# Layer-norm epsilon folded into VectorE's statistics, two biases moved from GpSimd adds into matmul accumulation, and all four engine orders rewritten, in a two-layer token tower

## What is computed

```python
h = concat(cls, patches @ W.T + b) + pos_enc                                   # tokens
x = ln(h); n = ln(x) * gamma + beta                                            # two norms, one after the other
z, c = sigmoid(n @ Wg.T + bg), n @ Wc.T + bc
h = h + scan(s = (1 - z) * s + z * c over an image's tokens) + x               # gated scan
h = h + (ln(gelu(ln(h) @ ternary(W_fc).T)) * ln_w + ln_b) @ ternary(W_proj).T  # first FFN
x = ln(h); q, k = rope(x @ Wq.T + bq), rope(x @ Wk.T + bk); v = x @ Wv.T + bv
h = h + (softmax(causal(q k / 16)) @ v) @ Wf.T + bf                            # attention
h = h + clip(round(ln(h) / scale)) * scale @ (ternary_weight - 1).T + bias     # quantized FFN
```

## Time and profile before

| | us |
|---|---|
| median of 3 runs | 164.12 |
| lowest, highest | 163.8, 164.88 |
| the profiled execution's own time | 163.71 |
| its span, first to last instruction | 161.9 |

### The profile page before, as it was taken

How to read it: one execution, slowest core, us unless ns; L and a number is a source line. 1 busy time by engine, 2 the same in 40 slices (tenths; PEclk the granted TensorE clock), 3 DMA queues, 4 the chain that set the end, 5 groups by cost and what they waited for, 6 DMA issues and landing times.

```text
span 161.9 us, 3532 instructions
## 1 busy us (share of the span) xinstructions
PE 148.2 (91%) x1043; PEld 129.5 (80%) x1043; DVE 136.1 (84%) x396; ACT 109.0 (67%) x264; POOL 120.3 (74%) x214
## 2 busy tenths in 40 slices
PE   7979999999998999999999999999999999697541
PEld 7969999788997887879888989988998798574220
DVE  0767679999999999999979799888988896896871
ACT  3765359736448899999998958498827637276330
POOL 1068978968927466878889988869899888988830
PEclk9999999999999999999999999999999999999955
DMA  5999992000030000000000000000000000001323
GB/s 171 340 392 392 379 417 109 4 0 2 0 130 4 2 0 2 0 4 0 0 4 2 0 4 0 2 0 0 4 0 0 0 6 2 2 10 46 87 81 81
DMA packets 6026, 10.84 MB, mean 67 GB/s; under 512 B 1841, under 2 KB 3448, under 8 KB 5752
## 3 DMA queue, kind: packets, MB, share of 16 engines
q1 hardware_dynamic: 6008, 10.62, 18.7%
HBM read 9.40 MB, written 1.21 MB: 66 GB/s over the span
## 4 chain that ended last, share of the span: by engine, by line
PE 70%; POOL 13%; DVE 6%; issue 6%; ACT 2%; DVEq 0%; ACTq 0%; POOLq 0%
PE bank L428 37%; PE bank L508 5%; PE bank L575 5%; PE bank L509 4%; PE bank L510 4%; PE bank L517 3%; POOL small L1186 3%; PE bank L435 3%; POOL qk L1251 2%; POOL small L1181 2%; POOL residual L1282 2%; POOL small L1191 2%; PE bank L549 1%; PE bank L629 1%; DVE residual L1160 1%
## 5 line engine op out<-in xcount | busy, mean ns | idle before, releaser
L1186 POOL TENSOR_TENSOR small<-small,powers 111x1 f32<-111x1 f32 (+3 forms) x55 | 33.3, 606 | 3.7
L1181 POOL TENSOR_SCALAR small<-small 111x1 f32<-111x1 f32 (+1 forms) x55 | 24.2, 441 | 15.0 <-DVE small L892 11.3
L428 PE MATMUL bank<-pj,gt_hi 128*111 128x256 f32 (+1 forms) x88 | 22.3, 293 | 0.0
L428 PE MATMUL bank<-pj,gt_lo 128*111 128x256 f32 (+1 forms) x88 | 21.3, 281 | 0.0
L1202 POOL TENSOR_TENSOR x_lo<-x_raw,x_hi 128x666 fp32r<-128x666 f32 (+1 forms) x9 | 12.8, 1434 | 10.8 <-ACT x_hi L721 10.8
L508 PE MATMUL bank<-wt_hi,x_hi 128*111 128x256 f32 (+1 forms) x66 | 19.4, 294 | 1.4 <-DVE h L998 1.1
L510 PE MATMUL bank<-wt_hi,x_lo 128*111 128x256 f32 (+1 forms) x66 | 18.6, 282 | 0.0
L509 PE MATMUL bank<-wt_lo,x_hi 128*111 128x256 f32 (+1 forms) x66 | 18.6, 282 | 0.0
L428 PE MATMUL bank<-fc,n1t_hi 128*111 128x512 f16 (+1 forms) x44 | 16.7, 380 | 0.0
L428 PE MATMUL bank<-fc,n1t_lo 128*111 128x512 f16 (+1 forms) x44 | 16.6, 378 | 0.0
L428 PEld LDWEIGHTS bank<-pj,gt_hi 128*111 128x111 f32 (+1 forms) x88 | 15.1, 171 | 0.3 <-DVE residual L1088 0.2
(11 more groups left out here) (139 smaller groups left out, 478.9 us busy)
## 6 DMA issues: line engine op xcount, KB each, us to landing
x_raw<-x_in SPq DMA_DIRECT2D x10, 333.0 KB, 6.4
w_fc<-w_fc_in SPq DMA_DIRECT2D x1, 1024.0 KB, 10.2
w_pj<-w_pj_in SPq DMA_DIRECT2D x1, 1024.0 KB, 12.2
out_dram<-residual SPq DMA_DIRECT2D x10, 96.0 KB, 1.7
w_tok<-w_tok_in SPq DMA_DIRECT2D x2, 384.0 KB, 4.1
w_gate<-w_gate_in SPq DMA_DIRECT2D x1, 512.0 KB, 5.8
w_qk<-w_qk_in SPq DMA_DIRECT2D x1, 512.0 KB, 7.0
ln_w<-ln_w_in SPq DMA_DIRECT2D x1, 512.0 KB, 3.5
```

The lines of the kernel that those rows point to most:

```text
L428: last = mm(out, a, b, start=(n == 0), stop=(n == len(pairs) - 1))
L1181: return nc.gpsimd.tensor_scalar(small[0:rows(i), i, out:out + 1], small[0:rows(i), i, value:value + 1], factor, add, ALU.mult, ALU.add)
L1186: return gt(small[0:rows(i), i, r:r + n], small[0:rows(i), i, ve:ve + n], powers[0:rows(i), 0:n], ALU.pow)
```

## The change

Four parts.

1. **Epsilon.** The statistics of a tile are six numbers, two groups of (count, mean, sum of squares). The tile `stats` becomes 12 wide, with two more groups of count 0 and mean 0 that POOL writes once at the start (`w_tok` on POOL: six memsets), whose sum of squares is 256 times epsilon. The aggregate reads nine numbers instead of six, and its variance is then variance + epsilon. `scaled` is gone for all norms: five instructions a tile on POOL. Norm 0 has two aggregates on DVE instead of one (`MV0_SQ`, `MV0`), one with e*e/(1 + e) and one with e; the factor 1/sqrt(1 + e) that is left goes into gamma (`w_gamma`, one small DVE instruction, for which `w_gate` on ACT and DVE waits). For norm 3, `NB3` is made of the mean, `R3` and -1/scale, and no longer waits for `RQ`.
2. **Value bias.** The tile `pick` (128 x 112) is 0 but for rows 0 and 32, which are 1. `value_rows` has the bias in all rows, rounded to fp32r, and in row 32 what the rounding left. Their product, 128 rows deep and 256 columns, is the first of now seven matmuls of `value:i`. `vbias` is gone on POOL, and DVE's `attend` doesn't wait for it. Two more instructions in `w_value_bias` on DVE.
3. **Output bias.** `out:i` on PE has the same product with `out_rows` (bias / scale) ahead of its two matmuls: three. `biased` is gone on POOL, and DVE's `out` doesn't wait for it. `w_out_bias` on POOL makes the rows once, in three instructions, after `h1:1`.
4. **Orders.** All four lists of `ORDER` are new. `w_pos:0` is behind `tok:0` on PE in both.

```diff
-                pairs = []
+                pairs = [(pick[0:STACK, 0:rows(i)], value_rows[0:STACK, :])]
...
+                mm(out[0:n, 0:D], pick[0:STACK, 0:n], out_rows[0:STACK, :], start=True, stop=False)
                 for k in range(KD):
-                    last = mm(out[0:n, 0:D], q3t[:, k, span(i)], w_out[:, k, :], start=(k == 0), stop=(k == KD - 1))
+                    last = mm(out[0:n, 0:D], q3t[:, k, span(i)], w_out[:, k, :], start=False, stop=(k == KD - 1))
...
-                    nc.vector.bn_aggr(col(i, normed[norm][2], 2), stats[0:rows(i), norm, i % 2, 0:6])\
-                        .then_inc(s[f"mv{norm}_ready"], 1)
+                    groups = stats[0:rows(i), norm, i % 2, :]
+                    if norm == 0:
+                        nc.vector.bn_aggr(col(i, MV0_SQ, 2), groups[:, 0:3 * GROUP]).then_inc(s["mv0_ready"], 1)
+                        nc.vector.bn_aggr(col(i, MV0, 2), groups[:, 0:4 * GROUP]).then_inc(s["mv0_ready"], 1)
+                    else:
+                        nc.vector.bn_aggr(col(i, normed[norm][2], 2), groups[:, 0:3 * GROUP])\
+                            .then_inc(s[f"mv{norm}_ready"], 1)
...
             def attend(i):
                 n = rows(i)
                 pool.wait_ge(s["mv3_ready"], i + 1)
-                scaled(i, VE3, MV3 + 1, 1.0, LN_EPS).then_inc(s["ve3_ready"], 1)
-                pool.wait_ge(s["ve3_ready"], i + 1)
-                power(i, VE3, R3).then_inc(s["r3_ready"], 1)
+                power(i, MV3, R3).then_inc(s["r3_ready"], 1)
...
-            def biased(i):
-                n = rows(i)
-                pool.wait_ge(s["s3_ready"], i + 1)
-                if i == 0:
-                    pool.wait_ge(s["dma_bias"], 16)
-                gt(res[0:n, i, :], res[0:n, i, :], out_bias[0:n, :], ALU.add).then_inc(s["biased_ready"], 1)
...
@@ the end of PE's list @@
-        turn:10 value:10 out:2 attend:10 out:3 out:4 t3:7 out:5 out:6 out:7 t3:8 out:8 t3:9 out:9 t3:10 out:10""",
+        out:3 turn:10 t3:5 out:4 t3:6 attend:10 t3:7 out:5 out:6 out:7 t3:8 out:8 t3:9 out:9 t3:10 out:10""",
```

More of the change, by code:

```diff
@@ new lines @@
+        tg:12 fc:17 t2:3 tg:13 fc:18 value:0 qk:0 tg:14 qk:1 tg:15 tg:16 fc:19 proj:6 t2:4 qk:2 tg:17 proj:7
+        t1:10 qk:3 tg:18 fc:20 t2:5 t2:6 proj:8 value:1 tg:19 t2:7 fc:21 score:0 score:1 qk:4 qk:5 tg:20 turn:0
+        proj:9 attend:0 qk:6 score:2 tg:21 turn:1 score:3 qk:7 value:2 turn:2 attend:1 t2:8 proj:10 value:3
+        value:4 t2:9 score:4 attend:2 score:5 turn:3 t2:10 value:5 attend:3 turn:4 qk:8 score:6 attend:4 qk:9
+        t3:0 turn:5 value:6 attend:5 turn:6 qk:10 score:7 attend:6 qk:11 value:7 t3:1 turn:7 out:0 t3:2 attend:7
@@ L322, in tower @@
     powers = m.own("powers", [2], F32)
-    stats = m.own("stats", [4, 2, 8], F32)
+    stats = m.own("stats", [4, 2, GROUP * GROUPS], F32)
     squares = m.own("squares", [HID], F16)
```

243 lines of the change are left out of this document (140 added, 103 removed).

## The result

| | median, us | lowest to highest, us | executions |
|---|---|---|---|
| before | 163.79 | 163.2 to 164.88 | 14 |
| changed | 163.0 | 161.93 to 165.76 | 14 |

The ratio is 0.9942, with a 95% interval of 0.9917 to 0.9967: 0.95 us faster (0.0058 x 163.79), where 1.8 were forecast. It is inside the range, and in the class "within 1%", which had a chance of 0.40 where "faster by over 1%" had 0.47. Executions more than 1.5% above their kernel's fastest stay out of every ratio in this document, while medians and ranges are of all executions, and since the profiled execution of the changed kernel was such a one (165.76 us), the profile after is that of its second run (first experiment), with a span of 160.8 us against 161.9.

The account below looks back on a forecast made before the run. PE was taken as the bound to about 130 us (with DVE up to 52), then a latency tail with POOL on the path. +0.8 + 1.75 - 1.6 - 2.7 = -1.8 us: 162.3 on the median, range 160.4 to 165.3.

Parts of the forecast that it names:

- Up to `attend:3`, +1.75: From 52 us to `attend:3`, PE without gaps: two more value stages, one score less, six bias products; +1.75 us.
- `attend:3` to `attend:10`, 18.8: In the tail on DVE: 17.8 us of work plus 1.0 idle, 18.8 instead of 20.4; -1.6 us.
- `attend:10` to the end, 9.2: The end: 3.9 us to the last `round`, 2.6 to the last `out`, 2.7 for stores; 9.2 instead of 11.9, -2.7.
- the hold on `clip`: In the tail: DVE's two `clip` took 1.60 us beside POOL's output adds; without them about 0.5.
- The first stage, +0.8: Up to about 52 us, new order and added DVE work: a loss between 0 and 1.7 us, taken as 0.8.
- two spots: In the first stage: PE waits 1.3 us at `t0:7`; `h1:0` behind its scan is 1.7 us late in all.
- the sign: Check for the first stage: right if PE's gaps between 30 and 52 us grow by about 0.8.
- the lock as a rival: DVE's `fc` and `pj` steps from about 31 us hold POOL's x_lo; PE stands 3.9 us; 165.4 us, chance 0.17.
- Its part on what is removed: 55 epsilon instructions and 22 adds leave POOL: worth nothing from 52 to 112 us, paying in the tail only.
- Another wait: Rival: the tail's idle stays at 3.8 us because another wait replaces POOL's; +1.05, 165.2 us, chance 0.18.
- Packs fully: Rival: the first stage loses 0.2, tail idle falls to 0.3, the end gives 3.1; -3.5, 160.6 us, chance 0.2.
- `w_out_bias`: On POOL after `h1:1`, near 53 us: at most 2.5 us long, costing nothing, up to 1 us if late.

Follow-up runs that it names:

- first experiment: The changed kernel run again with no edit, for a profile of an undisturbed execution: 163.03 us, ratio 0.995 to before.
- the old head: The changed code with all stages up to the first `t1` in the order of before, the later ones in the new order: 162.82 us, ratio 0.983.
- `code_old_order_new`: The kernel before with its own code, its lists replaced by the changed kernel's and the bias additions placed one or two tiles behind their norm: 175.94 us, ratio 1.075.

## Why the prediction was right, and where it was not

- **Up to `attend:3`, +1.75.** Measured +1.05 from `proj:0`. The parts that rows could check agree: the bias product at a spacing of 0.12, and no gap of PE. What made it 0.7 less was not looked for; in that stretch PE's order is different too, and part of the first stage's loss may be taken back there (`h1:0` was 4.15 us late and `proj:0` 3.16).
- **`attend:3` to `attend:10`, 18.8.** Measured 18.2. The idle time was forecast at 1.0 and is 1.1. DVE's work was forecast at 17.8 and is 17.06.
- **`attend:10` to the end, 9.2.** Measured 8.8. The forecast counted the last product at the low clock; the granted clock is 1.00 up to 158 us here, past that product (157.29), and from the end of the last `round` (156.29) to that of the last `out` (158.19) it is 1.9 us where 2.6 were counted. That the hold on `clip` would go was seen rightly.
- **The first stage, +0.8: this is the step that failed**, with +3.2 at `proj:0` (2.7 counted from `tok:1`). The prediction looked at two spots. Both have a wait: 0.51 us at `t0:7` and 0.64 at the scan, with 0.21 at the value bias 1.36 in all. But 1.10 us of gaps stood in this stretch before, so they grew by 0.26, and between 30 and 52 us, where growth by 0.8 was to be the sign, they fell from 1.10 to 0.72. What it left out is the 1.24 us at 27.78, and the 1.7 us of low clock behind it. It had the lock as a rival, with the right rows, but placed it only at the long steps for `fc` and `pj`, and judged by who is first there. It was right on that (POOL's x_lo at 33.65, DVE at 33.78), and missed that x_lo also holds the short ones, from which the epsilon instructions keep it away in the new order (26.47 with them, 24.65 without). Its part on what is removed prices POOL's relief at nothing where PE is full and gives it no price in the first stage; in the old head it is a loss of 0.4 to 0.6 us at `proj:0`, counted from `tok:1` and without a fall of the clock. In the new head it stands against the 1.31 us that PE waits for x_lo in `code_old_order_new`.
- **Rivals.** "Another wait" is true of the new code in the old order. "Packs fully" was nearer in the tail (-5.3 against its -5.4 and the forecast's -4.3). The sum came out between the forecast and no change because a tail 1.0 us better and a middle 0.7 better met a first stage 2.4 worse. That the total is so near is in part luck: three errors of which the largest is bigger than the forecast gain cancelled.
- **`w_out_bias`**, forecast at no more than 2.5 us, took 2.2 in the changed kernel (56.65 to 58.88). In the old order its cast was held (2.45 us instead of 0.40), and `h1:0` to `proj:0` took 23.7 us instead of 22.7; whether the one caused the other was not tested.
- **A row read too widely.** The lock rival took the 3.90 us of POOL at 35.01 for one hold over several DVE instructions. The row counts two instructions, and the first by itself took 2.37:

```profile
35.01 2.37 POOL L1181 TENSOR_SCALAR small<-small 111x1 f32<-111x1 f32 x1
```

It fits DVE's step for `fc` (35.00, 2.34 us), and the second fits that for `pj` (37.59, 1.27): one hold each. The traces show the longer hold on the other side, DVE's step for `fc` kept out through two x_lo in a row (33.78).

## What to carry to other kernels

Work taken from an engine that isn't the bottleneck moves its next instructions, and if it and another engine hold each other up, as GpSimd and VectorE do in these rows, it is where these land that decides: look for every long two-tensor instruction on GpSimd and ask what VectorE does in the 2 us behind its new start. An order written for one set of costs is part of the code: new code in the old order was 2.6% slower here, old code in the new order 7.5%, and both new 0.6% faster. A stand of PE may be paid a second time by the granted clock (1.24 us here, and 1.7 behind it), which only the windows show. And before two traces are compared by the times of landmarks, look for the first point that they share: here it moved by up to 1.2 us from one profile to another, as much as the effects that were sought.
